# Deformable convolution, image 0: image rows and corner table in parts, far rows last on one queue, indices in three parts

## The chip, the cores and the metric

One core of one Trainium2 chip runs the whole program. The metric is the device time of one execution in microseconds; the time of a kernel is the median of several executions.

## The reference

A batch of two images of 32 channels, 64 x 64 pixels, goes through four stages, each added to its input after a normalisation: a style normalisation with bicubic maps, a graph-like aggregation over 3 x 3 neighbours, a state-space scan over the 4096 tokens, and a deformable convolution. The change is in the last stage:

```python
def _L3_conv_ref(data_im, weight, offset_w, mask_w):
    offset = _conv(data_im, offset_w)                  # 18 values per pixel: y, x of 9 taps
    mask = jax.nn.sigmoid(_conv(data_im, mask_w))      # 9 values per pixel
    col = _deform_im2col(data_im, offset, mask)        # 4 corners of each tap, bilinear, times mask
    return jnp.einsum('op,bphw->bohw', weight, col)

x = x + _L2_conv_ref(_gn(x), ...)      # the scan
x = x + _L3_conv_ref(_gn(x), ...)
```

## The kernel before

Channels and image halves lie on the 128 partitions: rows 0 to 63 hold image 0 (two halves of 32 channels), rows 64 to 127 image 1. The scan of image 0 runs first, alone (`helped_*`, lines 1126 to 1195). Then image 0 is prepared for the deformable convolution (`prepare(0)`), and then the projection and scan of image 1 run on TensorE, VectorE and ScalarE, with the gathers of image 0 beside them on GpSimd. After the scan of image 1 comes `prepare(1)`, and the gathers of image 1 run beside sampling by matrix products of three of the nine taps (`dense_*`).

The 4096 pixels of an image are 32 groups of 128. For each group and tap, line 788 issues one indirect DMA that fetches for 128 pixels a row of 4 corners x 32 channels (512 bytes) from the corner table in HBM into one of five slots of `got`. `group_weigh` (line 792) on VectorE waits for a slot's gathers, copies the indices of five groups later into `idx_slot`, multiplies the slot by the coefficients (line 799, which frees the slot through `prod_done`), adds, and transposes for `group_multiply` on TensorE. GpSimd waits for `prod_done` ahead of a group (line 785). The turns of VectorE, TensorE and ScalarE are written into the projection (4 turns), the scan loop (5 turns an iteration), `prepare(1)` (turns 24 to 26 in its `between`) and what follows. Every engine runs its own list in order.

What `prepare(b)` does, by line:

- `vector` (1307): statistics, the normalised image `g4` (1317, `g_ready`), four transposes into the table's first corner (1322), two copies of the right neighbours (1326, 1328), and four copies of the lower right corner from PSUM (1332, `below_ready`). Then it waits for the image in G3 (1337), zeroes the edge columns (1338, 1339) and tells TensorE (`g3_ready`).
- `tensor` (1271): four products that shift the image down a row (1276), and the offset and mask convolution in two halves of 512 columns (1285), each of 4 quarters x 3 rows.
- `scalar` (1291): half of the image copies (1296), then the four copies of the lower corner into the table (1299).
- `sync` (1253): the other half of the image copies (1257), the table to HBM in two halves (1262), and after the convolution four copies of the residual into G3's place (1267).
- `load_image` (1247): three copies of a half image, one for each horizontal tap, shifted by a column.
- `positions` and `corners` (1345, 1351) take a half of the convolution out of PSUM and make indices of it; line 1359 tells GpSimd (`idx_ready`). Line 1364 copies the mask out (`mask_in`); the projection of image 1 on TensorE waits for that (line 912).

GpSimd starts when both hold:

```python
pool.wait_ge(l3["table_in"], 32 * (b + 1))    # 1590: both halves of the table are in HBM
pool.wait_ge(l3["idx_ready"], 2 * b + 1)      # 1591: indices of groups 0 to 15
```

## Time and profile before

| | us |
|---|---|
| median of 3 runs | 1004.47 |
| lowest and highest run | 1001.02, 1005.22 |
| the profiled execution | 999.45 |
| its span, first to last instruction | 997.5 |

| engine | busy us | share of the span |
|---|---|---|
| TensorE (PE) | 780.8 | 78% |
| VectorE (DVE) | 837.4 | 84% |
| ScalarE (ACT) | 375.1 | 38% |
| GpSimd (POOL) | 574.7 | 58% |

The table has shares over the whole span, which is made of stages with different limits. The chain that ended last tells which work set the end; the timeline tells what an engine's idle time ended with, in brackets behind an instruction; the windows tell the granted clock of TensorE (1.00 is 2.4 GHz, 0.50 is 1.2 GHz) and how busy the 16 DMA engines are in a stretch. Copies that SyncE or ScalarE issue stand as SPq and ACTq.

### The profile page before, as it was taken

To read this page: it belongs to the slowest core of one execution; us is meant where nothing else is said; L and a number is where in the kernel's file an instruction comes from. 1 tells how busy PE (TensorE), PEld (TensorE's weight loads), DVE (VectorE), ACT (ScalarE), POOL (GpSimd) and SP (SyncE) were. 2 spreads that over 40 slices of the span, in tenths; PEclk is the share of its full clock that TensorE was granted. 3 is DMA by queue.
4 is the path that set the end of the run, shared out by engine and by line. 5 is a ranking of instruction groups with operands and counts; after the bars stand their busy time and mean duration, and the time that the engine had idled before them with its cause. 6 is when DMAs were issued, how large, how long until landed. Compare 5 with 4: busy or idle time off the path is not lost.

```text
span 997.5 us, 8280 instructions
## 1 busy us (share of the span) xinstructions
PE 780.8 (78%) x2364; PEld 372.8 (37%) x2365; DVE 837.4 (84%) x1164; ACT 375.1 (38%) x535; POOL 574.7 (58%) x528
## 2 busy tenths in 40 slices
PE   3445878587778688778777887768389999999996
PEld 1122323132322134444343544414265444444443
DVE  3888853899999778689999999985989989989994
ACT  1120056854445135311111111101067777686640
POOL 0000000177674047777777777777777777777774
PEclk9666989789999798567777777777569999999998
DMA  5000018000000541111111112137343735444422
GB/s 124 0 0 1 0 32 170 5 0 1 0 1 0 106 104 48 47 51 50 50 52 50 50 50 53 50 97 186 105 138 90 206 113 148 135 126 114 124 66 53
DMA packets 32339, 69.82 MB, mean 70 GB/s; under 512 B 12368, under 2 KB 12624, under 8 KB 31184
## 3 DMA queue, kind: packets, MB, share of 16 engines
q1 hardware_dynamic: 16080, 35.27, 13.1%
q0 software_dynamic: 15360, 31.49, 12.2%
q10 hardware_dynamic: 864, 2.64, 1.2%
q8 instruction: 16, 0.26, 0.1%
q14 instruction: 19, 0.16, 0.0%
HBM read 54.94 MB, written 5.77 MB: 61 GB/s over the span
## 4 chain that ended last, share of the span: by engine, by line
POOL 48%; issue 17%; DVE 11%; PE 7%; ACT 1%; DMA 1%; POOLq 0%; ACTq 0%; SPq 0%; DVEq 0%
POOL got L788 47%; DVE scratch L1185 6%; DVE scratch L1192 3%; PE PS L1064 1%; PE PS L922 1%; DMA G<-XN 1%; PE PS L1285 1%; PE PS L923 1%; PE PS L931 1%; PE PS L1057 1%; PE PS L941 1%; PE PS L1049 1%; ACT scratch L1143 0%; PE PS L624 0%; DVE st L138 0%
## 5 line engine op out<-in xcount | busy, mean ns | idle before, releaser
L788 POOL DMA_INDIRECT got<-corner_table,idx_slot x405 | 401.7, 992 | 123.4 <-issue 123.4
L1049 PE MATMUL PS<-parts,selb 96*128 96x512 bf16 (+1 forms) x256 | 89.3, 450 | 78.4 <-DVE scratch L1111 41.0
L1064 PE MATMUL PS<-scratch,wt 128*128 128x512 f32 x256 | 149.9, 717 | 0.5 <-DVE scratch L1192 0.5
L1492 PE MATMUL PS<-scratch,UZ 128*128 128x512 f32 (+1 forms) x288 | 133.6, 613 | 2.9 <-DVE scratch L1477 2.9
L788 POOL DMA_INDIRECT got<-corner_table,idx_all x75 | 80.6, 1075 | 60.7 <-DVE prime L1359 38.1
L823 PE MATMUL PS<-ln_g,w 128*128 128x32 f32 x576 | 97.2, 334 | 0.0
L823 PEld LDWEIGHTS PS<-ln_g,w 128*128 128x128 f32 x576 | 94.5, 257 | 0.0
L829 ACT ACTIVATE G<-PS 128x32 f32 (+1 forms) x32 | 6.2, 195 | 221.4 <-PE PS L823 221.3
L1064 PEld LDWEIGHTS PS<-scratch,wt 128*128 128x128 f32 x256 | 59.9, 234 | 59.4 <-issue 50.1
L1161 POOL TENSOR_TENSOR scratch<-scratch 128x1024 f32<-128x1024 f32 x16 | 37.6, 2348 | 77.1 <-ACT scratch L1143 77.1
L1469 ACT ACTIVATE scratch<-UZ,knot 128x512 f32<-128x512 f32 (+1 forms) x128 | 81.6, 708 | 0.4
L1492 PEld LDWEIGHTS PS<-scratch,UZ 128*128 128x128 f32 (+1 forms) x288 | 53.2, 193 | 74.9 <-issue 56.1
L1049 PEld LDWEIGHTS PS<-parts,selb 96*128 96x128 bf16 x256 | 23.1, 118 | 154.1 <-DVE scratch L1111 55.1
L1576 POOL MEMSET w<- 128x1152 f32 x1 | 1.1, 1057 | 133.3 <-POOLq L318 133.3
L1111 DVE TENSOR_TENSOR_SCAN scratch<-scratch,carry,PS 128x1024 f32<-128x1024 f32 x32 | 75.1, 2347 | 1.1
L1492 PE MATMUL PS<-XN,UZ 128*128 128x512 f32 x144 | 65.2, 601 | 0.0
L1150 ACT ACTIVATE PS<-XN,negA 128x1024 f32<-128x1024 f32 x32 | 35.8, 1118 | 61.9 <-DVE scratch L1185 61.9
L1089 ACT ACTIVATE scratch<-XN,negA 128x1024 f32 x32 | 35.9, 1144 | 43.2 <-DVE XN L1103 34.5
L1477 DVE SCALAR_TENSOR_TENSOR scratch<-scratch,UZ 128x512 f32<-128x512 f32 (+1 forms) x72 | 45.5, 692 | 4.8 <-ACT UZ L1466 4.5
L1161 POOL TENSOR_TENSOR got<-scratch 128x1024 f32<-128x1024 f32 x16 | 37.6, 2349 | 16.8 <-ACT scratch L1143 16.8
L1477 DVE SCALAR_TENSOR_TENSOR XN<-XN 128x512 f32<-128x512 f32 (+1 forms) x72 | 45.4, 691 | 1.6 <-ACT XN L1466 1.4
L1477 DVE SCALAR_TENSOR_TENSOR scratch<-scratch,XN 128x512 f32<-128x512 f32 (+1 forms) x72 | 45.3, 689 | 0.3
(344 smaller groups left out, 1345.4 us busy)
## 6 DMA issues: line engine op xcount, KB each, us to landing
UZ<-dense_rows SPq DMA_DIRECT2D x24, 512.0 KB, 4.1
got<-corner_table,idx_slot POOLq DMA_INDIRECT x405, 2.5
UZ<-dense_rows SPq DMA_DIRECT2D x96, 64.0 KB, 2.2
XN<-ln_g SPq DMA_DIRECT2D x6, 256.0 KB, 5.1
got<-corner_table,idx_all POOLq DMA_INDIRECT x75, 2.6
corner_table<-scratch SPq DMA_DIRECT2D x1, 1056.0 KB
corner_table<-XN SPq DMA_DIRECT2D x1, 1056.0 KB
X<-in_x SPq DMA_DIRECT2D x4, 256.0 KB, 4.8
```

Of the source, the lines that this page charges most:

```text
L788: pool.indirect_dma_start(got[:, slot, tap, :, :].rearrange("p k c -> p (k c)"), None, tables[b], bass.IndirectOffsetOnAxis(ap=index[:, ta ...
L823: last = nc.tensor.matmul(group_psum(slot), w3[:, t, :], colgs[slot][:, t * C:t * C + C], start=False, stop=(t == n - 1))
L1049: last = nc.tensor.matmul(PS[:, first + n, :], selb[:, which, j, :], parts[:, bass.ds(i * CHUNK + n * BANK, BANK)], start=True, stop=True)
L1064: last = nc.tensor.matmul(PS[:, 4 + n, :], wt[:, W_SUM:W_SUM + P], dBC[:, j % 2, n * BANK:(n + 1) * BANK], start=False, stop=(j == PAIRS - 1))
L1089: nc.scalar.activation(dA[:, j % 2, :], dl[:, bass.ds(i * CHUNK, CHUNK)], ACT.Exp, scale=negA[:, j:j + 1]).then_inc(sc["exp_done"], 1)
L1111: tell(v, nc.vector.tensor_tensor_scan(hs, dA[:, j % 2, :], banks(0, 2), carry[:, j:j + 1], ALU.mult, ALU.add), sc["h_done"], s + 3)
L1150: nc.scalar.activation(banks(6, 2), dl[:, c * CHUNK:(c + 1) * CHUNK], ACT.Exp, scale=negA[:, j:j + 1]).then_inc(sc["exp_done"], 1)
L1161: nc.gpsimd.tensor_tensor(dBu[j % 2], dus[c % 2], Bs[j % 2], ALU.mult).then_inc(sc["dbu_done"], 1)
L1185: tell(v, nc.vector.tensor_tensor_scan(hs, banks(6, 2), dBu[j % 2], carry[:, j:j + 1], ALU.mult, ALU.add), sc["h_done"], s + 3)
L1469: nc.scalar.activation(ramps[k][rows, j, :], loads[k][rows, 1, :], ACT.Relu, bias=knot[rows, j:j + 1]).then_inc(de["ramps"], 1)
L1477: nc.vector.scalar_tensor_tensor(ramps[k][rows, j, :], ramps[k][rows, j, :], 1.0, hats[k][rows, :], ALU.min, ALU.mult).then_inc(de["prods" ...
L1492: last = nc.tensor.matmul(PS[:, n % 4, :], steps[rows, j, :, :].rearrange("p b c -> p (b c)"), ramps[k][rows, j, :], start=(j == 0), stop= ...
```

## The change

For image 0 alone:

- The image rows go into G3 in two steps. First the near rows (in each quarter of 16 rows the first three and the last), from SyncE and ScalarE, with a semaphore of their own, `g3_near`; then the far rows (12 of 16), all from SyncE, behind the table.
- The table goes to HBM in four parts instead of two, for both images; the copies of the right neighbours are in four parts and stand between the transposes.
- The convolution and the indices are made in parts of 4, 12 and 16 groups. The first needs the near rows alone. VectorE waits for the far rows after the indices of the first part. Image 1 keeps two parts of 16 groups and whole image copies.
- GpSimd waits for the second part of the indices ahead of group 4. Semaphore counts change accordingly.

```diff
@@ -713,6 +713,7 @@
         gathered = [sem(f"gathered{k}") for k in range(SLOTS)]
+        g3_near = sem("g3_near")
@@ -1228,6 +1229,9 @@
+        TABLE_PARTS = ((0, 15), (15, 31), (31, 47), (47, W))
+        NEAR_ROWS, FAR_ROWS = ((0, 3), (15, 16)), ((3, 15),)
+
         def prepare(b):
@@ -1244,29 +1248,44 @@
-            def load_image(engine, h):
-                for j in range(3):
-                    first = W + h * HALF - (j - 1)
-                    engine.dma_start(G3[32 * j:32 * j + 32, first:first + HALF],
-                                     g4[64 * b + 32 * h:64 * b + 32 * h + 32, :]).then_inc(l3["g3_in"], 16)
+            PARTS = ((0, 4), (4, 16), (16, 32)) if b == 0 else ((0, 16), (16, 32))
+            parts_before = 3 * b
+
+            def load_image(engine, h, row_ranges=((0, HALF // W),)):
+                for first_row, last_row in row_ranges:
+                    for j in range(3):
+                        first = W + h * HALF - (j - 1)
+                        lo, hi = first_row * W, last_row * W
+                        if len(row_ranges) == 1 and last_row < HALF // W:
+                            lo, hi = lo + (j == 2), hi - (j == 0)
+                        n = HALF // 2 if last_row < HALF // W else HALF
+                        engine.dma_start(G3[32 * j:32 * j + 32, first:first + HALF].rearrange("p (q n) -> p q n", n=n)[:, :, lo:hi],
+                                         g4[64 * b + 32 * h:64 * b + 32 * h + 32, :].rearrange("p (q n) -> p q n", n=n)[:, :, lo:hi]
+                                         ).then_inc(l3["g3_in"] if last_row - first_row > 3 else g3_near, 16)
             def sync(sp):
...
                 sp.wait_ge(l3["g_ready"], b + 1)
-                load_image(sp, 0)
-                for k, (first, last) in enumerate(((0, W // 2 - 1), (W // 2 - 1, W))):
-                    sp.wait_ge(l3["right_ready"], 2 * b + k + 1)
-                    sp.wait_ge(l3["below_in"], 4 * b + 2 * k + 2)
-                    sp.wait_ge(l3["below_ready"], 4 * b + 2 * k + 2)
+                if b == 0:
+                    load_image(sp, 0, NEAR_ROWS)
+                else:
+                    load_image(sp, 0)
+                for k, (first, last) in enumerate(TABLE_PARTS):
+                    sp.wait_ge(l3["right_ready"], 4 * b + k + 1)
+                    sp.wait_ge(l3["below_in"], 4 * b + k + 1)
+                    sp.wait_ge(l3["below_ready"], 4 * b + k + 1)
                     sp.dma_start(tables[b].rearrange("(y x) n -> y x n", y=H)[:, first:last, :].rearrange("y x n -> y (x n)"),
                                  tab[rows, first:last, :, :].rearrange("p x k c -> p (x k c)")).then_inc(l3["table_in"], 16)
-                sp.wait_ge(l3["off_psum"], 2 * b + 2)
+                if b == 0:
+                    for h in range(2):
+                        load_image(sp, h, FAR_ROWS)
+                sp.wait_ge(l3["off_psum"], parts_before + len(PARTS))
                 for q in range(4):
...
                                  X[first:first + 32, q % 2 * QUARTER:q % 2 * QUARTER + QUARTER]).then_inc(l3["resid_in"], 16)
-                sp.wait_ge(l3["table_in"], 32 * (b + 1))
+                sp.wait_ge(l3["table_in"], 64 * (b + 1))
             def tensor(pe, between=nothing):
@@ -1277,13 +1296,15 @@
-                pe.wait_ge(l3["g3_ready"], b + 1)
-                for n in range(2):
+                for k, (lo, hi) in enumerate(PARTS):
+                    if k < 2:
+                        pe.wait_ge(l3["g3_ready"], 2 * b + min(k, 1 - b) + 1)
+                    n, lo, hi = lo // 16, 32 * (lo % 16), 32 * ((hi - 1) % 16 + 1)
                     for q in range(4):
...
                             first = q * QUARTER + n * BANK + dy * W
-                            last = nc.tensor.matmul(PS[32 * q:32 * q + 32, 4 + n, :], wt[0:96, W_OFF + 32 * dy:W_OFF + 32 * dy + 32],
-                                                    G3[:, first:first + BANK], start=(dy == 0), stop=(dy == 2))
+                            last = nc.tensor.matmul(PS[32 * q:32 * q + 32, 4 + n, lo:hi], wt[0:96, W_OFF + 32 * dy:W_OFF + 32 * dy + 32],
+                                                    G3[:, first + lo:first + hi], start=(dy == 0), stop=(dy == 2))
                     last.then_inc(l3["off_psum"], 1)
@@ -1293,7 +1314,10 @@
                 act.wait_ge(l3["g_ready"], b + 1)
-                load_image(act, 1)
+                if b == 0:
+                    load_image(act, 1, NEAR_ROWS)
+                else:
+                    load_image(act, 1)
                 for n in range(4):
@@ -1317,15 +1341,20 @@
-                for n in range(4):
+                def corner(n):
                     xs = slice(16 * n, 16 * n + 16)
...
                                         ).then_inc(l3["corner_ready"], 1)
+
+                def right(k):
+                    lo, hi = TABLE_PARTS[k]
+                    hi = min(hi, W - 1)
+                    v.wait_ge(l3["corner_ready"], 4 * b + min(k + 1, 4))
+                    nc.vector.tensor_copy(tab[rows, lo:hi, 1, :], tab[rows, lo + 1:hi + 1, 0, :]).then_inc(l3["right_ready"], 1)
+
+                corner(0), corner(1)
                 nc.vector.memset(tab[rows, W - 1, 1::2, :], 0.0)
-                v.wait_ge(l3["corner_ready"], 4 * b + 2)
-                nc.vector.tensor_copy(tab[rows, 0:W // 2 - 1, 1, :], tab[rows, 1:W // 2, 0, :]).then_inc(l3["right_ready"], 1)
-                v.wait_ge(l3["corner_ready"], 4 * b + 4)
-                nc.vector.tensor_copy(tab[rows, W // 2 - 1:W - 1, 1, :], tab[rows, W // 2:W, 0, :]).then_inc(l3["right_ready"], 1)
+                right(0), corner(2), right(1), corner(3), right(2), right(3)
                 for n in range(4):
@@ -1334,36 +1363,52 @@
                 cols = G3.rearrange("p (y x) -> p y x", x=W)
-                v.wait_ge(l3["g3_in"], 96 * (b + 1))
-                vchain(v, nc.vector.memset(cols[0:32, :, 0], 0.0))
-                tell(v, nc.vector.memset(cols[64:96, :, W - 1], 0.0), l3["g3_ready"], b + 1)
+                if b == 0:
+                    edges = [cols[32 * j:32 * j + 32, 1:H + 1, x].rearrange("p (q r) -> p q r", r=16) for j, x in ((0, 0), (2, W - 1))]
+                    v.wait_ge(g3_near, 16 * 12)
+                    vchain(v, nc.vector.memset(cols[64:96, 0:1, W - 1], 0.0))
+                    vchain(v, nc.vector.memset(cols[0:32, H + 1:H + 2, 0], 0.0))
+                    vchain(v, nc.vector.memset(edges[0][:, :, 0:3], 0.0))
+                    vchain(v, nc.vector.memset(edges[0][:, :, 15:16], 0.0))
+                    vchain(v, nc.vector.memset(edges[1][:, :, 0:3], 0.0))
+                    tell(v, nc.vector.memset(edges[1][:, :, 15:16], 0.0), l3["g3_ready"], 1)
+                else:
+                    v.wait_ge(l3["g3_in"], 96 * 2)
+                    vchain(v, nc.vector.memset(cols[0:32, :, 0], 0.0))
+                    tell(v, nc.vector.memset(cols[64:96, :, W - 1], 0.0), l3["g3_ready"], 3)
                 between(0)
...
-                def positions(half):
-                    part = slice(16 * half, 16 * half + 16)
-                    v.wait_ge(l3["off_psum"], 2 * b + half + 1)
-                    vchain(v, nc.vector.transpose(om[:, part, :].rearrange("p g k -> p (g k)"), PS[:, 4 + half, :]))
+                def positions(k):
+                    part, half = slice(*PARTS[k]), PARTS[k][0] // 16
+                    v.wait_ge(l3["off_psum"], parts_before + k + 1)
+                    vchain(v, nc.vector.transpose(om[:, part, :].rearrange("p g k -> p (g k)"),
+                                                  PS[:, 4 + half, 32 * (part.start % 16):32 * ((part.stop - 1) % 16 + 1)]))
                     vchain(v, nc.vector.tensor_tensor(yx[:, part, :], om[:, part, 0:18], bases[:, part, :], ALU.add))
-                def corners(half):
-                    part = slice(16 * half, 16 * half + 16)
+                def corners(k):
+                    part = slice(*PARTS[k])
                     vchain(v, nc.vector.tensor_scalar(corner0[:, part, :], yx[:, part, :], 0.5, 0.0, ALU.subtract, ALU.max))
...
                         corner0[:, part, 0::2], float(W), corner0[:, part, 1::2], ALU.mult, ALU.add))
-                    nc.vector.memset(prime[:, 12 + 2 * b + half:13 + 2 * b + half], 0.0).then_inc(l3["idx_ready"], 1)
-
-                positions(0)
-                corners(0)
-                positions(1)
+                    nc.vector.memset(prime[:, 10 + 2 * b + k:11 + 2 * b + k], 0.0).then_inc(l3["idx_ready"], 1)
+
+                for k in range(len(PARTS)):
+                    if k:
+                        corners(k - 1)
+                    if b == 0 and k == 1:
+                        v.wait_ge(l3["g3_in"], 16 * 6)
+                        vchain(v, nc.vector.memset(edges[0][:, :, 3:15], 0.0))
+                        tell(v, nc.vector.memset(edges[1][:, :, 3:15], 0.0), l3["g3_ready"], 2)
+                    positions(k)
                 tell(v, nc.vector.tensor_copy(msk, om[:, :, 18:27]), l3["mask_in"], b + 1)
                 between(1)
-                corners(1)
+                corners(len(PARTS) - 1)
@@ -1587,9 +1632,11 @@
                     first = b * GROUPS
-                    pool.wait_ge(l3["table_in"], 32 * (b + 1))
-                    pool.wait_ge(l3["idx_ready"], 2 * b + 1)
+                    pool.wait_ge(l3["table_in"], 64 * (b + 1))
+                    pool.wait_ge(l3["idx_ready"], 3 * b + 1)
                     for G in range(first, first + SLOTS):
+                        if G == 4:
+                            pool.wait_ge(l3["idx_ready"], 2)
                         group_gather(pool, b, G, G % SLOTS, idx_all[:, G * TAPS:(G + 1) * TAPS])
```

## Rows read from the trace of the kernel before

**Rows 1.** The page, part 4: the chain that ended last, shares of the span

```profile
POOL 48%; issue 17%; DVE 11%; PE 7%; ACT 1%; DMA 1%; POOLq 0%; ACTq 0%; SPq 0%; DVEq 0%
```

**Rows 2.** Groups by line, POOL, 358 to 987: busy us, mean ns, idle before

```profile
L788 POOL DMA_INDIRECT got<-corner_table,idx_slot x405 | 401.7, 992 | 123.4 <-issue 123.4
L788 POOL DMA_INDIRECT got<-corner_table,idx_all x75 | 80.6, 1075 | 60.7 <-DVE prime L1359 38.1 <-issue 22.5
```

**Rows 3.** Timeline of POOL: start, us, instruction, idle before it, releaser

```profile
358.52 1.12 POOL L788 DMA_INDIRECT got<-corner_table,idx_all  x1 [38.11 <-DVE prime L1359]
```

**Rows 4.** The chain in order of time, 338 to 358: start, us, what

```profile
338.83 7.76 DMA G<-XN
346.69 0.12 DVE G L1338
346.92 0.12 DVE G L1339
347.08 7.73 PE PS L1285 x28
357.70 0.82 issue
```

**Rows 5.** Windows: busy of PE, PEld, DVE, ACT, POOL, PEclk, DMA share, GB/s

```profile
336.00:338.00 2.00, 0.00 (x0) 0.00 (x0) 1.97 (x3) 0.00 (x0) 0.00 (x0) 0.50 0.00 0
338.00:346.00 8.00, 7.09 (x8) 1.63 (x8) 6.06 (x11) 2.52 (x5) 0.00 (x0) 0.50 0.99 199
347.00:352.00 5.00, 4.92 (x12) 1.10 (x14) 0.03 (x1) 0.10 (x1) 0.00 (x0) 0.52 1.00 206
348.00:356.00 8.00, 8.00 (x40) 2.24 (x40) 1.03 (x2) 0.00 (x0) 0.00 (x0) 0.76 0.96 199
352.00:358.00 6.00, 6.00 (x39) 1.88 (x34) 2.47 (x7) 0.00 (x0) 0.00 (x0) 1.00 0.66 138
```

**Rows 6.** DMA issues by line: count, KB each, median us to landing

```profile
corner_table<-scratch SPq DMA_DIRECT2D x1, 1056.0 KB
corner_table<-scratch SPq DMA_DIRECT2D x1, 992.0 KB
G<-XN SPq DMA_DIRECT2D x3, 256.0 KB, 5.3
w<-in_wts SPq DMA_DIRECT2D x12, 4.0 KB, 1.7
```

**Rows 7.** Timeline, all engines, 337 to 347: copies issued and last table copies

```profile
337.00 2.71 SPq L1250 DMA_DIRECT2D G<-XN  x3
337.06 4.13 ACTq L1250 DMA_DIRECT2D G<-XN  x3
341.96 1.25 DVE L1332 COPY scratch<-PS 64x480 f32<-64x480 f32 x2
345.83 0.68 DVE L1332 COPY scratch<-PS 64x512 f32<-64x512 f32 x1 [1.02 <-ACT scratch L1299]
```

**Rows 8.** Timeline of DVE: transposes of both index halves and the mask copy

```profile
354.94 0.72 DVE L1348 STREAM_TRANSPOSE scratch<-PS 128x512 f32<-128x512 f32 x1 [7.91 <-PE PS L1285]
358.39 0.72 DVE L1348 STREAM_TRANSPOSE scratch<-PS 128x512 f32<-128x512 f32 x1 [0.74 <-PE PS L1285]
359.63 0.31 DVE L1364 COPY XN<-scratch 128x288 f32<-128x288 f32 x1
```

**Rows 9.** Waits of DVE, 358 to 700: us in total, times, longest

```profile
DVE idx_slot L796 <- DMA got<-corner_table,idx_all: 4.6, 3, 2.4
```

**Rows 10.** Timeline of DVE and POOL: group 26's product, group 31's first gather

```profile
713.37 1.35 DVE L799 TENSOR_TENSOR prodg<-got,coef 128x1152 f32<-128x1152 f32 x1
726.93 1.60 POOL L788 DMA_INDIRECT got<-corner_table,idx_slot  x1 [0.30 <-issue]
```

**Rows 11.** Waits of DVE, 700 to the end: us in total, times, longest

```profile
DVE idx_slot L844 <- DMA got<-corner_table,idx_slot: 11.0, 5, 4.4
DVE prodg L846 <- DMA got<-corner_table,idx_slot: 6.2, 3, 3.5
```

More of the change, by code:

```diff
@@ L1004, in preactivation @@
                 if b == 1 and c == 0:
-                    v.wait_ge(l3["table_in"], 32)
+                    v.wait_ge(l3["table_in"], 64)
                 nc.vector.tensor_scalar(log_tmps[b][:, cols], banks(4, 2), V(V_BDT), 20.0, ALU.add, ALU.min).then_inc(pr["clamp_done"], 1)
@@ L1458, in dense_scalar @@
                 act.wait_ge(de["tables_in"], 32)
-                act.wait_ge(l3["table_in"], 32 * B)
+                act.wait_ge(l3["table_in"], 64 * B)
             act.wait_ge(load[k], 16 * (n // RING + 1))
```

## The prediction

> **What bounds the kernel now.** I read the chain that ended last first: almost half of the span is GpSimd (POOL), and nearly all of that is line 788, the gathers of the deformable convolution [rows 1]. Next the groups of that line: 480 gathers, 482 us busy, and before them only 0.3 us pauses called issue plus one wait of 38.1 us, for L1359, the marker that indices are ready [rows 2]. That wait ends at 358.52 [rows 3]. So from 358.52 to the last gather POOL never waits for a free slot, for the second corner table or for anything else; it issues one gather per 1.31 us (482 us busy and 146 us of pauses, by 480). The end of the kernel moves with the moment of the first gather, one for one, as long as POOL keeps having no wait.
>
> What sets 358.52? The chain in order of time [rows 4]: the six image copies into G3 land at 346.59 (338.83 plus 7.76), two edge memsets, the offset convolution, 7.73 us for its first half, the index arithmetic and its marker, and from 357.70 on 0.82 us between POOL's release and the first gather. The table is a second condition and no earlier by much: the DMA engines run full at 199 GB/s for the image (338 to 346) and at the same 199 GB/s for the table (348 to 356) [rows 5]. Image 6 x 256 KB and table 992 + 1056 KB [rows 6] are 3.67 MB, at 199 GB/s 18.4 us, from 338.2 to 356.6. The table thus lands about 1 us ahead of the indices. Both conditions must move for POOL to start sooner.
>
> **The change, part by part.**
>
> *Near rows first.* Twelve small copies (48 KB and 16 KB in turn, 384 KB in all) take the place of six; six per queue. The issues cost SP 2.71 us for three and ACT 4.13 us [rows 7], the later ones slowed since the DMA engines are full. Small weight loads land 1.7 us after issue [rows 6]. SP's mean was 0.90 us an issue, ACT's 1.38. I take 0.6 us, since the near copies don't fill the engines, and 2 us to land: 337.0 + 6 x 0.6 + 2 = 342.6. Bounds: 341.7 (half of SP's mean) and 347.3 (ACT's mean). It is hidden up to 346.5, since DVE is busy with the last copy of the table until 345.83 + 0.68 [rows 7]; if the issues took ACT to 345.3, its four table copies would come late by 4 us, and with them the table.
>
> Here a rule of the Trainium skill speaks against the change. The row above says that 4 KB to 12 KB copies land in 1.7 us while several are in flight [rows 6]. "DMA: Bandwidth & Descriptors", section "Rules for kernel authors", says that transfers under 64 KB are mostly overhead, and its "Specifications" put line rate at 512 B per run and more; the near rows are 48 KB with runs of 768 B and 16 KB with runs of 256 B. Taken so that each holds its queue for its own 2 us, the near rows would land near 349; that outcome is a rival below, priced from rows.
>
> *Table in four parts, ahead of the far rows.* A part may go when its own quarter is copied. The first `below` copy ended near 342.6 (two from 341.96, 1.25 us) [rows 7]; two more and smaller right-neighbour copies ahead of it add some 0.4 us, so the first part is issued at 343.1. Flow starts about 1.1 us after an issue (issued at 337.00, nothing up to 338, full after) [rows 5, 7], at 344.2. The later parts are ready by 346.5, before the queue has got to them. 2.10 MB at 199 GB/s is 10.5 us: last byte 354.7, with 0.3 us for the completion 355.0, and 0.85 us to the first gather: **355.9 instead of 358.5, 2.6 us earlier**. Bounds 1.7 (first part 0.5 us later, completion 0.7 us) to 3.5 (both without loss).
>
> *Indices in parts of 4, 12 and 16 groups.* Six memsets 0.23 us apart [rows 4] instead of two: the convolution starts at 348.0. A quarter of the columns of a half that took 7.73 us, mostly at the low clock, is about 2.5 us; bounded above by 5 us if weight loads set the pace. The arithmetic on a quarter is some 1.6 us instead of 2.9. Indices at 352.1, at the latest 354.7: still ahead of the table. So the table is what POOL waits for, and the gain of the index path beyond 355.0 is worth nothing.
>
> *Far rows behind the table.* This is the price. Six copies, 1152 KB, 5.9 us at 199 GB/s, behind the table on SP's queue: 354.7 + 5.9 + 0.4 (first gathers beside them) = 361.0. DVE waits for them in order (it did not wait there before), then two memsets, then PE starts the other 28 groups at 361.6. Queued behind that wait are everything of image 1 on DVE and, through `mask_in`, PE and ACT. PE has paused ten us; after a like pause it ran at a granted 0.5 and went to 1.00 within 5 us of the convolution's start [rows 5]. At full clock a half took 3.45 us (354.94 to 358.39) [rows 8], so at 0.5 twice that; the first half, which ramps up, took 4.8 us low plus 2.9 us full. Three quarters of it and the second half: 7.5 us all at full clock, 15.0 us all at half. With 4.8 us at half, as before, it is 9.9 us: 371.5, then transpose, add and mask copy (1.7 us by the second half's rows, which ended at 359.94) [rows 8]: 373.2. **Image 1 starts 13.3 us later** (10.9 to 18.4). The second convolution part is on no path of POOL: groups 0 to 3 keep it busy for 36 x 1.31 = 47 us. The residual copies, next on SP, go out some 12 us later too; the first product that needs them comes later by as much. ACT has no far copies to issue any more; its next work, the table's lower corner, waits for PE anyway.
>
> *What that delay does.* DVE then waited 4.6 us in three places for gathers [rows 9]; it will come later and the gathers earlier, so these go: net 8.7 us (6.3 to 13.8). POOL reuses a slot after DVE weighed it. Of all 59 reuses the tightest is group 26's slot: product done at 713.37 + 1.35 = 714.72, group 31's first gather at 726.93 [rows 10], 12.2 us of room. It shrinks by 2.6 + 8.7 = 11.3: POOL just doesn't wait. From 700 on DVE stood 17.2 us waiting for gathers [rows 11]; it makes up its 8.7 us there and ends with POOL.
>
> *The rest.* Image 1's table in four parts, its index parts and other semaphore counts: its table is wanted at 739, over 40 us after it lands; zero. Gathers take 0.99 us in the steady part and 1.08 us in the 75 that read their indices from `idx_all`, which run beside DVE's preparations [rows 2]. The same DVE work will meet them, plus some 5 us more: up to 0.5 us lost; on the other side DVE is idle beside the first nine, 9 x 0.08 = 0.7 us gained. I take zero.
>
> Sum: 2.6 us. The profiled execution took 999.45 (span 997.5 plus 2 around it), so 996.9; the median of the runs stands 5.0 above it, at 1004.47, and the same step gives 1001.9.
>
> **The rivals.**
>
> *The slot ring binds (ends on the other side).* If image 1 comes later by more than 12.2 us net of the 4.6, POOL waits before group 31 and its start no longer counts. With the split convolution all at half clock (15.0 us) the net delay is 13.8: the end is 13.8 - 12.2 = 1.6 us later than before, 1006.1; some 2.5 us more if the scan meets low clock too, 1008.6. For it: 0.9 us of room left in my sum, and a clock that restarts at 0.5. Against: before, the clock rose 5 us into the same convolution.
>
> *The start does not move.* The near copies clog both queues, or ACT's table copies come late behind six issues: first part issued at 345.5 (ACT's mean) to 348 (near rows one after another), first gather 2.4 to 4.9 us later than in the sum, at 358.3 to 360.8: no change to 2.3 us slower, 1004.3 to 1006.8. It is also the case in which the change doesn't do what it says. For it: 4.13 us for three issues on ACT; against: those were held by full DMA engines.
>
> *More than the sum.* Table flow at 343.5 and gathers at their best pace while DVE is idle: 3.5 + 0.7 = 4.2 us, 1000.3.
>
> **How the numbers follow.** Forecast 0.5, ring 0.25, start unmoved 0.13, more 0.12. A measurement of this kernel tells 0.5% (5 us) from no change, and none of the cases reaches that by itself: faster needs the last case with the runs' spread (1001.02 to 1005.22), 0.12; slower needs the ring with a slow scan, 0.09; same 0.79. Range: 998 (the fourth case, less the 2 us by which runs scatter) to 1008 (the ring case near its bound).
>
> **What would show it.** First gather at 355.2 to 356.8, released by the table's landing and no longer by the index marker; the DMA rate unbroken from 344 through 361; three blocks of the offset convolution, the second from about 361.6 at a granted 0.5 at first; the mask copy near 373; no idle time of POOL over 0.3 us at group 31, where a wait would name a DVE product. The prediction is wrong if the first gather starts after 358, if the scan of image 1 starts over 12 us later, or if POOL waits between image 0's last groups.

## The result, and the profile after

| | before | after |
|---|---|---|
| median of 20 runs | 1003.69 | 1008.82 |
| lowest and highest run | 1000.65, 1007.91 | 1004.83, 1012.29 |
| profiled execution, its span | 999.45, 997.5 | 1005.60, 1003.6 |
| normalised image ready (first transpose into the table) | 337.00 | 338.13 |
| first gather | 358.52 | 356.82 |
| mask copy of image 0 | 359.63 | 374.08 |
| scan of image 1 starts | 413.30 | 424.72 |
| last gather issued (its end) | 986.81 | 991.15 |

The ratio is 1.0050, 95% interval 1.0039 to 1.0062: about 5 us slower, where 2.6 us faster had been forecast and 1008 was the upper end of the range. The stages ahead of the change ended 1.1 us later in the trace of after; moments within the preparation are therefore counted below from the first transpose into the table, at 337.00 and 338.13. Both profiled executions lie below the medians of their kernels, by 4.2 and 3.2 us.

The shares of the chain that ended last, the view of [rows 1]:

```profile
PE 42%; DVE 34%; issue 5%; ACT 2%; SPq 1%; DMA 1%; DVEq 1%; POOL 0%; ACTq 0%; POOLq 0%
```

Before, this chain was GpSimd's (POOL 48%). After, POOL is not on it: the end hangs on TensorE and VectorE, that is on image 1. The preparation of image 0, from the timelines of SyncE's queue, VectorE, TensorE and POOL (start, us, instruction, idle time before it and its releaser), the view of [rows 3, 7, 8]:

```profile
338.13 3.89 SPq L1262 DMA_DIRECT2D G<-XN  x6
343.97 5.41 SPq L1278 DMA_DIRECT2D corner_table<-scratch  x4
352.94 0.06 DVE L1399 MEMSET prime<- 128x1 f32 x1
356.82 1.12 POOL L789 DMA_INDIRECT got<-corner_table,idx_all  x1 [35.28 <-DMA corner_table<-scratch]
362.48 0.10 DVE L1406 MEMSET G<- 32x48 f32 x1 [9.48 <-DMA G<-XN]
362.83 9.97 PE L1306 MATMUL PS<-G,wt 96*32 96x384 f32 x48 [11.61 <-DVE G L1407]
374.08 0.31 DVE L1409 COPY XN<-scratch 128x288 f32<-128x288 f32 x1
```

The first gather is now released by the table, 18.69 us after the first transpose instead of 21.52. The far rows keep VectorE waiting for 9.5 us, the rest of the convolution starts at 362.83, and the mask copy comes 13.3 us later. Then the gathers, grouped by line (busy us, mean ns, idle before), the view of [rows 2]:

```profile
L789 POOL DMA_INDIRECT got<-corner_table,idx_slot x405 | 405.6, 1001 | 123.4 <-issue 122.8 <-DVE prodg L847 0.6
L789 POOL DMA_INDIRECT got<-corner_table,idx_all x75 | 82.8, 1104 | 57.8 <-DMA corner_table<-scratch 35.3 <-issue 22.6
```

They were busy 482.3 us before and are 488.4 us now; from the first to the last it takes 634.3 us instead of 628.3. POOL waited for slots only 0.6 us in all. Last, group 26's product and the first gather of group 31, the view of [rows 10]:

```profile
721.17 1.35 DVE L800 TENSOR_TENSOR prodg<-got,coef 128x1152 f32<-128x1152 f32 x1
730.26 0.98 POOL L789 DMA_INDIRECT got<-corner_table,idx_slot  x1 [0.30 <-issue]
```

Here 7.7 us of room are left of 12.2. The waits of VectorE from 700 to the end (us in total, times, longest), the view of [rows 11]:

```profile
DVE prodg L847 <- DMA got<-corner_table,idx_slot: 5.4, 2, 4.1
DVE UZ L1564 <- PE PS L1554: 5.0, 2, 2.8
DVE scratch L1522 <- ACT UZ L1511: 4.8, 1, 4.8
DVE idx_slot L845 <- DMA got<-corner_table,idx_slot: 4.4, 2, 2.5
DVE XN L1548 <- PE PS L1554: 3.0, 1, 3.0
```

Its 17.2 us of waiting for gathers have become 9.8, and waits for TensorE (L1554) stand beside them with 8.0 us, against 2.1 before (at L1509). Why TensorE does not catch up, the windows of its last stretch show (columns as in [rows 5]), first before, then after, 8 us later:

```profile
740.00:860.00 120.00, 120.00 (x373) 55.24 (x371) 112.20 (x198) 90.18 (x151) 91.97 (x92) 1.00 0.49 138
860.00:986.00 126.00, 126.00 (x373) 55.31 (x372) 109.94 (x195) 70.61 (x119) 95.94 (x99) 1.00 0.37 106
```

```profile
748.00:868.00 120.00, 120.00 (x373) 55.24 (x371) 114.24 (x202) 90.27 (x151) 91.97 (x93) 1.00 0.49 138
868.00:994.00 126.00, 126.00 (x373) 55.31 (x372) 108.18 (x192) 70.64 (x119) 93.89 (x97) 1.00 0.37 105
```

TensorE is busy for all of these 246 us at the full clock, the same 746 matmuls in both. It had no pause to give back, and what delays its start delays its end: the last sampling product ended 8.1 us later (986.3 and 994.4). Before, the last gather landed 2 us behind that product, so only 2 us of the delay were covered. These are the lines, of before and after for TensorE, and of before for VectorE's product of the last gather:

```profile
984.42 1.90 PE L1509 MATMUL PS<-XN,UZ 128*32 128x512 f32 x4
992.52 1.90 PE L1554 MATMUL PS<-XN,UZ 128*32 128x512 f32 x4
988.34 0.96 DVE L846 TENSOR_TENSOR prodg<-got,coef 128x768 f32<-128x768 f32 x1 [1.29 <-DMA got<-corner_table,idx_slot]
```

### The profile page after: what moved, and what is told of

Same layout as the page of the kernel before. It is cut to its first block, busy times and chain, and to the rows that moved or that the text cites. A ratio compares the mean times of both kernels' runs of the same rounds, so it can differ in the third digit from the quotient of the medians.

```text
span 1003.6 us, 8367 instructions
## 1 busy us (share of the span) xinstructions
PE 781.5 (78%) x2389; PEld 371.4 (37%) x2389; DVE 838.6 (84%) x1181; ACT 375.2 (37%) x535; POOL 580.8 (58%) x528
## 3 DMA queue, kind: packets, MB, share of 16 engines
q1 hardware_dynamic: 17216, 35.86, 13.4%
q10 hardware_dynamic: 1200, 2.05, 0.9%
## 4 chain that ended last, share of the span: by engine, by line
PE 42%; DVE 34%; issue 5%; ACT 2%; SPq 1%; DMA 1%; DVEq 1%; POOL 0%; ACTq 0%; POOLq 0%
PE PS L1537 19%; DVE scratch L1112 7%; DVE scratch L1186 5%; PE PS L824 3%; DVE PS L1109 3%; DVE scratch L1193 3%; DVE prodg L800 3%; PE PS L1554 2%; PE PS L1065 2%; PE PS L864 2%; PE PS L1306 2%; DVE prodg L804 2%; PE PS L1050 2%; PE PS L1295 1%; PE PS L932 1%
## 5 line engine op out<-in xcount | busy, mean ns | idle before, releaser
L1065 PE MATMUL PS<-scratch,wt 128*128 128x512 f32 x256 | 153.0, 730 | 0.5 <-DVE scratch L1193 0.5
L789 POOL DMA_INDIRECT got<-corner_table,idx_all x75 | 82.8, 1104 | 57.8 <-DMA corner_table<-scratch 35.3
L824 PE MATMUL PS<-ln_g,w 128*128 128x32 f32 x576 | 92.9, 325 | 0.0
L824 PEld LDWEIGHTS PS<-ln_g,w 128*128 128x128 f32 x576 | 90.1, 247 | 0.0
```

The lines of the kernel that those rows point to most:

```text
L789: pool.indirect_dma_start(got[:, slot, tap, :, :].rearrange("p k c -> p (k c)"), None, tables[b], bass.IndirectOffsetOnAxis(ap=index[:, ta ...
L824: last = nc.tensor.matmul(group_psum(slot), w3[:, t, :], colgs[slot][:, t * C:t * C + C], start=False, stop=(t == n - 1))
L1065: last = nc.tensor.matmul(PS[:, 4 + n, :], wt[:, W_SUM:W_SUM + P], dBC[:, j % 2, n * BANK:(n + 1) * BANK], start=False, stop=(j == PAIRS - 1))
```

## The experiments

All are compared with the kernel before by the ratio on record for their runs, with its interval; 0.1% is 1.0 us. It is not quite the quotient of the medians, which is 1.0076 for e1, 1.0043 for e13 and 1.0068 for e14. Single traces of image 1's scan differ by more than any effect here: its first two chunks of four took 116.7 to 125.7 us, with the same instructions. So times are told by ratios, traces tell where a wait stands. "Scan" is the start of image 1's scan after the first transpose, against the kernel before; "3 to 5" is the time from the first gather of group 3 to that of group 6; "tail" is what follows the last gather's issue.

| kernel | ratio, 95% interval | first gather | scan | 3 to 5 | tail |
|---|---|---|---|---|---|
| before | 1 | 21.52 | 0 | 37.17 | 10.72 |
| after | 1.0050, 1.0039 to 1.0062 | 18.69 | +10.3 | 41.91 | 12.46 |
| e1 delay 13 | 1.0057, 1.0035 to 1.0079 | 22.30 | +11.8 | 41.71 | 13.63 |
| e7 delay 6.7 | 1.0042, 1.0025 to 1.0060 | 21.46 | +3.2 | 40.69 | 10.55 |
| e15 delay 3.3 | 1.0030, 1.0018 to 1.0043 | 21.51 | +3.2 | 39.12 | 12.00 |
| e2 far rows first | 1.0039, 1.0021 to 1.0057 | 24.54 | +4.7 | 39.52 | 10.30 |
| e9 parts only | 0.9995, 0.9981 to 1.0009 | 22.33 | -0.1 | 35.97 | 11.06 |
| e13 before, GpSimd 3 us late | 1.0036, 1.0019 to 1.0053 | 25.45 | +3.0 | 36.36 | 10.34 |
| e14 after, GpSimd 3 us late | 1.0058, 1.0044 to 1.0071 | 21.65 | +10.0 | 40.69 | 12.79 |
| e3 before, light | 0.9992, 0.9975 to 1.0009 | 21.55 | -1.3 | 35.81 | 10.76 |
| e4 after, light | 1.0019, 1.0005 to 1.0034 | 18.68 | +10.4 | 41.72 | 10.61 |
| e6 swap | 1.0052, 1.0032 to 1.0073 | 18.68 | +10.5 | 40.72 | 13.58 |
| e10 fill | 1.0070, 1.0049 to 1.0091 | 18.69 | +12.5 | 38.27 | 13.39 |
| e12 light and fill | 1.0030, 1.0013 to 1.0046 | 18.69 | +12.5 | 38.25 | 10.86 |
| e5 tokens early | 1.0044, 1.0028 to 1.0061 | 20.32 | +9.9 | 42.49 | 10.75 |
| e8 tokens and swap | 1.0068, 1.0047 to 1.0088 | 20.33 | +11.2 | 41.28 | 10.73 |
| e11 tokens and fill | 1.0085, 1.0064 to 1.0106 | 20.34 | +12.3 | 38.35 | 13.79 |

### Is it the delay of image 1? (e1, e7, e15)

The kernel before with nothing but memsets on VectorE, 12, 6 or 3 of them, ahead of the second half of the indices:

```diff
+                if b == 0:
+                    for _ in range(12):
+                        vchain(v, nc.vector.memset(prodg[:, :, :, :].rearrange("p t k c -> p (t k c)"), 0.0))
                 positions(1)
```

> The kernel before, with 12 chained memsets of 128x1152 on VectorE between the first and the second half of image 0's indices: about 13 us in which image 1 is held up, and nothing else of the change. Theory 1 (image 1's delay reaches the end through TensorE, whose sampling products ran from 737 to 986 us without a pause): 13 less 4.6 us of waits for gathers that go, less 2 us by which TensorE was done ahead of the last gather, so 6 to 7 us slower than before. Theory 0, that of the prediction (the end moves with the gathers alone): no change, since the slot with the least room has 12.2 us. Theory 2 (the end is late because the gathers themselves became slower as VectorE runs without gaps): 0 to 6 us, and then with POOL's gathers longer in sum by as much.

> The kernel before with 6 chained memsets of 128 x 1152 on VectorE between the indices of groups 0 to 15 and the rest of the preparation of image 0: image 1 starts about 6.7 us later, GpSimd's first gather stays. Theory 'image 1's delay costs, through the gathers' pace and through TensorE': slower gathers in groups 3 to 5 (38 to 42 us against 37.2), time 1 to 5 us over the kernel before, less than the 7.6 of twice the delay. The forecast's theory (GpSimd alone sets the end, and VectorE makes up 8.7 us): no difference.

> The kernel before with three memsets of 128 x 1152 (3.3 us) on VectorE ahead of the second half of image 0's indices; image 1 starts 3.3 us later. By the cost of 6.7 us (3.7) and of 13.1 us (7.6), which lie on one line through the origin of 0.57 us for each, 1.5 to 2.2 over the kernel before. If TensorE's room of 2 us and VectorE's early waits cover a small delay, 0 to 1. The forecast's theory: no difference.

The delay alone costs as much as the whole change: the mask copy came 15.9, 7.1 and 3.2 us later, and the time rose by 5.7, 4.2 and 3.0, with image rows and table as in the kernel before (the first gather came 0.8 us later in e1 and within 0.1 us in the others). The forecast's "no difference" falls. So does the idea that TensorE's 2 us would cover the small one; between the smaller two the intervals don't tell a difference, nor do their scans, which both start 3.2 us later. In e1 the chain of waits is the one of after:

```profile
PE 46%; DVE 29%; issue 5%; ACT 2%; DMA 1%; POOL 1%; DVEq 1%; ACTq 0%; SPq 0%; POOLq 0%
```

### Is it the parts, or the order? (e9, e2)

e9 is the kernel before with index parts alone, whole image first; e2 is the changed kernel with the far rows right behind the near rows.

```diff
+            PARTS = ((0, 4), (16, 32), (4, 16)) if b == 0 else ((0, 16), (16, 32))
...
+                        if G == 4:
+                            pool.wait_ge(l3["idx_ready"], 3)
```

```diff
                     load_image(sp, 0, NEAR_ROWS)
+                    load_image(sp, 0, FAR_ROWS)
...
                     load_image(act, 1, NEAR_ROWS)
+                    load_image(act, 1, FAR_ROWS)
```

> The kernel before with one part of the change alone: convolution and indices of image 0 in parts, groups 0 to 3 first, then 16 to 31, then 4 to 15; the image rows are loaded whole and ahead of the table as before, the table goes in two halves, GpSimd waits for the last part ahead of group 4. First gather released by the table's landing or the first indices, 1 to 2.5 us earlier than before; mask copy 0.5 to 2 us later. Theory 'image 1's delay is what costs': no delay worth the name, so gathers of groups 3 to 5 near 37 us (36 to 39), and the time 0 to 2 us below the kernel before. Theory 'the parts themselves, or any change of phase, cost': 2 to 5 us above. The forecast's theory: 1 to 2.5 below.

> The changed kernel with the far rows issued right behind the near rows, by both queues, ahead of the table. All else of the change stays (four table parts, three index parts). The far rows land near 348, so image 1 is held up by 1 us at most; the table lands near 357 and the first gather starts at 358, about as before. Theories 1 and 2: within 2 us of before, since the far rows' wait is gone. If the four table parts, the smaller copies or the index parts cost the time: 3 to 6 us slower, as the change was.

The parts cost nothing: 0.9995. They gain nothing either, and the trace of e9 says why: the first indices are ready early, and POOL waits for the table.

```profile
353.13 0.06 DVE L1366 MEMSET prime<- 128x1 f32 x1
360.92 1.12 POOL L788 DMA_INDIRECT got<-corner_table,idx_all  x1 [38.93 <-DMA corner_table<-scratch]
```

The table, behind the whole image, lands no earlier than the indices of the kernel before are ready, so here the first gather comes sooner if image rows go behind the table, which is what delays image 1. e2 missed its expectation: 3.9 us slower. With eighteen image copies in place of six, ScalarE issued until 344.6 (341.2 before) and made its table copies after that; the first gather came at 24.54, the mask copy 5.7 us late.

### What is the first gather worth? (e13, e14)

Three memsets on GpSimd ahead of the first gather, in the kernel before and in the changed one:

```diff
+                    for k in range(3 if b == 0 else 0):
+                        nc.gpsimd.memset(got[:, SLOTS - 1, 0:8, :, :].rearrange("p t k c -> p (t k c)")[:, 0:1000], 0.0).then_inc(l3["w3_zero"], 1)
+                        pool.wait_ge(l3["w3_zero"], 6 + k)
```

> The kernel before with three chained memsets of 128 x 1000 on GpSimd, about 3 us, behind its waits and ahead of the first gather of image 0; nothing else moves. This prices the first gather by itself, in the direction opposite to the change. The forecast's theory (the end moves with the first gather, microsecond for microsecond): 2.5 to 3.5 us over the kernel before. Theory 'image 1's path through VectorE and TensorE ends as late': 0 to 1.5 over. If VectorE then waits more for gathers in groups 3 to 5 and these run freely, less than the 3 us.

> The changed kernel with the same 3 us on GpSimd ahead of the first gather, so that the gathers start as late as in the kernel before, while image 1 still starts 13 us late. If the earlier first gather is worth its 2.8 us, 1.5 to 3.5 us over the changed kernel (that is 7 to 8 over the kernel before, as with the pure delay of image 1 by 13 us, 7.6); if TensorE's path hides it, within 1 us of the changed kernel.

In the kernel before, a first gather 3.9 us later costs 3.6 us: the time fits the forecast's rule. The trace does not: image 1 was late too, since VectorE waited 7.3 us for gathers in the projection and the scan started 3.0 us later, and the chain that ended last was TensorE's. So e13 does not price the first gather alone. In the changed kernel 3.0 us cost 0.8 (1.0058 against 1.0050), less than either interval is wide (1.6 by the medians); that the early gather is worth nothing there is not shown, but the chain had no share of POOL. The chains of e13 and e14:

```profile
PE 45%; DVE 23%; POOL 8%; issue 6%; ACT 2%; DMA 1%; DVEq 0%; ACTq 0%; SPq 0%; POOLq 0%
PE 44%; DVE 31%; issue 5%; ACT 2%; SPq 1%; DMA 1%; DVEq 1%; POOL 0%; ACTq 0%; POOLq 0%
```

### Does TensorE set the end of the changed kernel? (e3, e4)

Both kernels with 5 of the 9 sampling products of each batch; part of the sum is left out.

```diff
-            for j in range(SLOPES):
+            for j in range(0, SLOPES, 2):
```

> The kernel before with five instead of nine products in each of the 24 sampling batches on TensorE (the even slopes alone; VectorE and ScalarE still make all nine weights), so part of the sum of three taps is left out. TensorE gets some 80 us of room in the last 250 us. The end should then be that of the gathers: 0 to 1 us faster than before by all theories, since before the last gather landed 2 us behind TensorE's last sampling product.

> The changed kernel with the same four of nine products left out of each sampling batch. Theory 1 with gathers at their old pace: 2.6 us faster than the kernel before, the gain of the earlier first gather. Theory 1 with slower gathers (6 us more in the profiled run): 2 to 4 us slower than before, and about 2 us faster than the changed kernel. Theory 2 (gathers alone set the end): as slow as the changed kernel, 5 us over before.

The kernel before does not gain beyond its interval; the changed kernel comes down from 5.0 to 1.9 us over. TensorE then waits 25.4 us for VectorE (waits of PE, 740 to 994, in e4), and the tail is 10.6 again:

```profile
PE PS L1537 <- DVE scratch L1522: 25.4, 17, 6.5
```

So about 3 of the 5 us go when TensorE has room. The other 2 stay, with gathers as slow as in the changed kernel: in e4's trace they take 5.4 us longer than before and start 2.8 us earlier, 2.6 us in sum.

### Why are the gathers slower? (e6, e10, e12)

In every kernel whose image 1 is late against its first gather, but for those with the memset below, the gathers of groups 3 to 5 take 39 to 42 us instead of 37; in e13, where both are late together, they take 36.4. One of them in the changed kernel, timelines of POOL and of VectorE:

```profile
408.09 1.31 POOL L789 DMA_INDIRECT got<-corner_table,idx_all  x1 [0.30 <-issue]
409.71 3.51 POOL L789 DMA_INDIRECT got<-corner_table,idx_all  x1 [0.30 <-issue]
413.52 0.98 POOL L789 DMA_INDIRECT got<-corner_table,idx_all  x1 [0.30 <-issue]
```

```profile
409.85 1.20 DVE L1022 TENSOR_TENSOR parts<-scratch,parts 32x1024 bf16<-32x1024 f32 x1
410.98 0.15 DVE L797 COPY idx_slot<-idx_all 128x9 uint32<-128x9 uint32 x1
411.06 1.34 DVE L800 TENSOR_TENSOR prodg<-got,coef 128x1152 f32<-128x1152 f32 x1
412.43 0.76 DVE L804 TENSOR_TENSOR prodg<-prodg 128x576 f32<-128x576 f32 x1
413.22 0.46 DVE L807 TENSOR_TENSOR ln_g<-prodg 128x288 f32<-128x288 f32 x1
```

The gather of 3.51 us begins just ahead of L1022 and ends at 413.22, 0.82 us after L800: VectorE runs these two operations, each with two operands in SBUF, with no gap in which the gather got through. Before, VectorE stood here waiting for gathers [rows 9]; that those waits kept its products in step with them fits the traces, e13's too, where VectorE waits. e6 puts an operation with an operand in PSUM ahead of the weighing; e10 puts a short memset there, for groups 1 to 3; e12 is e10's edit in the light kernel (the same part of the sum left out).

```diff
-            low(0), left(2), low(1)
+            if b == 1:
+                low(0), low(1), left(2)
+            else:
+                low(0), left(2), low(1)
```

```diff
+            if isinstance(G, int) and G in (1, 2, 3):
+                vchain(v, nc.vector.memset(prodg[:, :, :, :].rearrange("p t k c -> p (t k c)")[:, 0:512], 0.0))
             v.wait_ge(gathered[slot], arrived)
```

> The changed kernel with one exchange in image 1's projection on VectorE: the subtraction with an operand in PSUM (left(2)) goes behind the two subtractions with both operands in SBUF (low(0), low(1)) instead of between them, so that it stands right ahead of the weighing of a group. No work is added or left out. Theory 'operations with two operands in SBUF, back to back, hold GpSimd's gather up': the gather that took 3.51 us in three of four kernels with a late image 1 falls below 2.5, groups 3 to 5 take 39 to 41 us instead of 41.9, and the time falls by 0.5 to 2. Theory 'the gathers are slower by chance of phase': their sum stays within 0.5 us, the time too. If TensorE alone sets the end, the gathers fall and the time does not.

> The changed kernel with a memset of 128 x 512 (about 0.5 us, no operand read) on VectorE ahead of the weighing of groups 1, 2 and 3 of image 0, which in the changed kernel followed an operation with two operands in SBUF without a gap. Theory 'back-to-back operations with two SBUF operands hold the gather up': the gather of 3.51 us falls below 2.5 and groups 3 to 5 take 37 to 40 us instead of 41.9, although VectorE has 1.5 us more to do; the time falls by 0 to 2 (TensorE's path, a little later, becomes the end). If the hold-up has another cause, the gathers stay within 0.7 us of 41.9 and the time does not fall.

> The changed kernel with 5 of the 9 sampling products of a batch left out (part of the sum is missing; TensorE then waits for the others), which alone came out 2.3 us over the kernel before, plus the memset of 128 x 512 on VectorE ahead of the weighing of groups 1 to 3. TensorE's path is out of the way here, so what the memset gives back of the gathers must show in the time: 1.5 to 3.5 us below the kernel with the products left out alone, about level with the kernel before (-1.5 to +1). If the gathers' pace does not set the end there, no difference from 2.3 over.

The swap fails: the gather that began ahead of the weighing still took 3.29 us, so an operand in PSUM is not enough. Why not stays open: in the scan, operations with an operand in PSUM hold no gather up (last section). The memset works on the gathers: none in these groups is over 1.9 us, and they take 38.3 us instead of 41.9. The same place in e10, POOL and VectorE:

```profile
413.12 0.94 POOL L789 DMA_INDIRECT got<-corner_table,idx_all  x1 [0.30 <-issue]
414.36 1.76 POOL L789 DMA_INDIRECT got<-corner_table,idx_all  x1 [0.30 <-issue]
413.26 0.48 DVE L796 MEMSET prodg<- 128x512 f32 x1
413.96 1.35 DVE L802 TENSOR_TENSOR prodg<-got,coef 128x1152 f32<-128x1152 f32 x1
```

And yet no time is gained: 1.0070. Image 1 became another 2.2 us later, and TensorE sets the end (tail 13.4). With TensorE out of the way, in e12, the gathers' gain of 3.5 us is lost at another place, where POOL now waits for a slot (waits of POOL from 600 on):

```profile
POOL got L789 <- DVE prodg L802: 3.4, 1, 3.4
```

That is the prediction's first rival, the slot ring, and the wait stands ahead of group 31, where it had been placed: when the gathers run ahead, the late image 1 stops them.

### Can image 1 be started sooner? (e5, e8, e11)

The changed kernel with six of image 1's eight token blocks made while TensorE waits for the far rows; e8 adds e6's edit, e11 e10's.

```diff
+                    if b == 0 and k == 0:
+                        project_tensor(pe, 1, early=True)
...
+            if b == 1:
+                tokens(6), tokens(7)
+                pe.wait_ge(l3["mask_in"], 1)
+                delta(0)
+                between(0)
+                delta(1), delta(2)
```

> The changed kernel; TensorE and ScalarE make the first token blocks of image 1's projection (blocks 0 to 5 of 8) between the first and the second part of image 0's convolution, where TensorE stood idle for 10 us waiting for the far rows, and blocks 6 and 7 behind the convolution, so that only the delta products wait for the mask copy. First gather, mask copy and table as in the changed kernel (2.8 us earlier and 13 us later than before, counted from the normalised image). Theory 'image 1's delay costs, through the gathers' pace and through TensorE': the delta products start 7 us earlier than in the changed kernel, the scan starts 3 to 8 us later than in the kernel before instead of 11.4, and the time is 2 to 5 us below that of the changed kernel, that is 0 to 3 above the kernel before. Theory 'the table in four parts or the parts themselves cost': the time stays within 1 us of the changed kernel's 5.1 over the kernel before. The forecast's theory (GpSimd alone sets the end): 1.5 to 3 us below the kernel before.

> Both edits in one: token blocks early, and the subtraction with an operand in PSUM right ahead of the weighing of a group. If both costs are real and independent, 0.5 to 2 us below the kernel with the token blocks alone, about level with the kernel before (-2 to +2); if the swap does nothing, equal to it.

> The changed kernel with both costs reduced: token blocks 0 to 5 of image 1 made in TensorE's idle time between the parts of image 0's convolution (that alone left the time 3.8 us over the kernel before, with GpSimd's last gather setting the end), and a memset of 128 x 512 on VectorE ahead of the weighing of groups 1 to 3 (that alone gave back 3.6 us of the gathers and nothing of the time, with TensorE setting the end). If the end is the later of GpSimd's path and TensorE's, and both edits keep their effect, 1 to 3 us over the kernel before, that is 2 to 4 below the changed kernel. If one of the two paths was not real, no better than the better of the two edits alone (3.8 over).

The blocks were done early, and the scan started no sooner (+9.9): VectorE makes the coefficients of image 0 until 384 (385 in the changed kernel) and takes the first delta products only then. TensorE, ahead of it, stood for 9.9 us and came back at the low clock. Windows 384 to 404, after and then e5; the eighth column is the granted clock:

```profile
384.00:404.00 20.00, 18.70 (x58) 8.77 (x57) 16.20 (x18) 12.23 (x16) 15.33 (x16) 1.00 0.19 53
```

```profile
384.00:404.00 20.00, 14.61 (x34) 6.39 (x34) 12.97 (x15) 4.99 (x5) 15.19 (x16) 0.65 0.20 52
```

In e5 the chain that ended last was GpSimd's again:

```profile
POOL 48%; issue 16%; DVE 11%; PE 7%; ACT 1%; DMA 1%; POOLq 0%; SPq 0%; DVEq 0%; ACTq 0%
```

Its first gather came 1.2 us earlier than before and its gathers took 633.0 us instead of 628.3, so in this trace their pace, not TensorE, made the end late. e8 (1.0068) is no better, and e11 was the slowest of all. Its memsets put the scan at +12.3, and POOL waited 5.9 us for a slot. No edit tried here gave a version that beats the kernel before.

## Why the prediction was wrong

**Right: the preparation.** First gather 2.83 us earlier (2.6 forecast), released by the table; near rows landed 5.5 us after the first issue (5.6); image 1 13.3 us later (13.3); VectorE's 4.6 us of waits for gathers gone; the scan of image 1 10.3 us later (8.7 forecast, bounds 6.3 to 13.8). The rival that the start does not move is out. (One reading there goes beyond its row: [rows 6] has copies of 4 KB at 1.7 us; those of 12 KB took 2.1.) The Trainium skill, "DMA: Bandwidth & Descriptors", "Rules for kernel authors", says that under 64 KB a transfer pays mostly overhead. Taken as in that rival, each copy holding its queue for 2 us, the near rows would have landed 12 us after the first issue; here the overheads overlapped, one copy landing every 0.3 us over the two queues.

**Wrong: "it makes up its 8.7 us there and ends with POOL".** For VectorE there was such room. TensorE had none: the windows show it busy without a pause for 246 us up to its last sampling product in both kernels, a view that the prediction does not use. The chain's share for PE, 7% [rows 1], tells that it was not last, not by how much; it was 2 us. This is the step that failed: the sampling ended 8.1 us later, and 8.1 less 2.0 is what the trace of after is longer, 6.1 us. e1, e7 and e15 show that a delay alone costs as much as the change, and e4 that about 3 of the 5 us go when TensorE has room. None of the prediction's three signs of being wrong came up; none of them looks at TensorE.

**Wrong in size: "Gathers ... I take zero", bounds 0.5 lost and 0.7 gained.** Measured: 6.0 us lost over 480 gathers, 4.7 of them in groups 3 to 5. By itself this term would have turned the 2.8 us gained at the start into 3.2 lost. The prediction saw that VectorE's waits would vanish and booked that as a gain; with them went the pauses that, as e10's memset suggests, kept its products out of the gathers' way.

**Wrong as a rule: "one for one, as long as POOL keeps having no wait".** The time of e13 fits it (3.6 us for 3.9), but by its trace the end was TensorE's, so the fit may be luck; in the changed kernel e14 gives 0.8 for 3.0, though POOL had almost no waits there either.

**The slot ring** did not bind in the changed kernel, as forecast, but for another reason: 7.7 us of room were left where 0.9 had been summed up, because the gathers themselves came later. In e11 and e12 it bound, for 5.9 and 3.4 us.

**What stays open.** Over the kernels with all products, the ratio follows the start of image 1's scan (no delay 0.9995, about +3 us 1.0030 to 1.0042, +10 to +12 us 1.0044 to 1.0085). How much of the 5 us is TensorE's stretch and how much the gathers' pace can't be split cleanly: both paths ended later (by the two traces 6.1 and 3.2 us), and taking one away lets another set the end, the gathers in e5, the slot ring in e12. Why the scan's pace differs by up to 9 us between single traces was not found.

## What to carry to other kernels

Before a piece of work is put off, look for the last engine that it feeds and see in the windows whether that engine has any pause left until the end; an engine that is busy without a gap passes a delay on, even if the chain of waits does not run through it. A wait that disappears is not always a gain: it may have kept two engines in step. And the chain that ended last does not say by how much it was last; here it was 2 us.

## What the hardware showed

A gather of GpSimd is held up by VectorE's operations with two operands in SBUF. In the seventeen traces together, 606 gathers began inside a weighing product, at least 0.1 us behind its start and 0.3 us ahead of its end. All of them took longer than the usual 0.94 us, up to 2.05, and ended 0.81 to 0.83 us after the product. Of the 1705 that began likewise inside the scan's operations with an operand in PSUM, none took more than 0.96 us. Two operations with both operands in SBUF, back to back, can hold one gather together: 0.94 us became 3.51, from 0.14 us ahead of L1022 to 0.82 us after L800.

It depends on who is first. Of image 0's gathers, the 134 that began 0.17 to 0.25 us ahead of a weighing product took 0.95 us at most; of the 16 that began 0.12 to 0.16 us ahead, nine took 2.28 to 2.33. The Trainium skill, "SBUF — State Buffer", "SBUF: two separate sides", says that of a VectorE operation with two SBUF inputs and a GpSimd operation that reads SBUF, whichever starts first holds a shared pair of ports for the whole instruction. For the gathers the traces agree, but for these nine and the one of 3.51 us, which all began a little ahead and still waited.
